# Row sums of a global attention spread by DMA copies in place of a matmul, with the steps behind them one slot later

## What is computed

```python
x = x + L0_conv_ref(_gn(x), ...)        # neighbourhood attention, 7x7 windows, 16 heads of 8 channels
t = _to_tokens(x)                       # (8, 3136, 128)
t = t + L1_attn_ref(_ln_t(t), ...)      # global attention, 8 heads of 16 channels, softmax over 3136 keys
t = t + L1_ffn_ref(_ln_t(t), ...)       # two linear maps without bias, the first one dequantised
x = _from_tokens(t, x)
```

## Time and profile before

| | |
|---|---|
| median of 3 runs | 9302.65 us (9293.14 to 9307.9) |
| span of the profiled execution | 9305.0 us |
| instructions | 435888 |
| mean granted TensorE clock, share of full speed | 0.979 |
| TensorE matmuls busy | 8705.1 us (94%), 173512 instructions |
| VectorE busy | 7484.8 us (80%) |
| ScalarE busy | 6697.0 us (72%) |
| GpSimd busy | 2837.7 us (30%) |
| DMA | 257.48 MB, mean 28 GB/s |

### The profile page before, as it was taken

One profiled execution on the slowest core, in us unless ns is written; L12 is line 12 of the kernel. 1 busy time (PEld: TensorE's weight loads), 2 busy tenths in 40 slices (PEclk: granted clock), 3 DMA queues, 4 the chain that ended last, 5 costly groups with the idle time before them and its releaser, 6 DMA issues.

```text
span 9305.0 us, 435888 instructions
## 1 busy us (share of the span) xinstructions
PE 8705.1 (94%) x173512; PEld 4692.7 (50%) x173512; DVE 7484.8 (80%) x13786; ACT 6697.0 (72%) x14241; POOL 2837.7 (30%) x2805
## 2 busy tenths in 40 slices
PE   5799999999999999999999999999999999999998
PEld 4445554555545555455554555545555455554543
DVE  6588888888787787888778877888778878789985
ACT  2377777777777777777777777777777777777777
POOL 5524441244303343034330343303432134320000
PEclk8899999999999999999999999999999999999999
DMA  1110101101011010110002000020011200011000
GB/s 44 45 43 20 28 25 41 26 21 27 24 43 26 18 28 24 48 25 20 23 25 55 16 21 24 25 52 17 22 27 27 49 14 25 25 27 30 8 11 8
DMA packets 312360, 257.48 MB, mean 28 GB/s; under 512 B 97244, under 2 KB 303052, under 8 KB 308300
## 3 DMA queue, kind: packets, MB, share of 16 engines
q1 hardware_dynamic: 310348, 229.05, 10.1%
HBM read 136.82 MB, written 78.05 MB: 23 GB/s over the span
## 4 chain that ended last, share of the span: by engine, by line
PE 87%; issue 5%; DVE 3%; ACT 2%; POOL 2%; DMA 1%; SPq 0%; ACTq 0%; DVEq 0%; POOLq 0%
PE PS L1156 23%; PE PS L1224 23%; PE PS L1209 22%; PE PS L966 6%; PE PS L1024 5%; PE PS L1032 4%; PE PS L1042 3%; ACT PB L1440 1%; DVE block_max L1694 1%; PE PS L1016 1%; PE PS L1072 1%; PE PS L998 0%; DVE X L1618 0%; DMA vT_padded<-SC 0%; DVE NM L1565 0%
## 5 line engine op out<-in xcount | busy, mean ns | idle before, releaser
L1694 DVE TENSOR_REDUCE block_max<-PS 128x1 f32<-128x448 f32 x10862 | 6160.8, 617 | 1098.6 <-PE PS L1156 1023.1
L1440 ACT ACTIVATE PB<-PS 128x448 f32<-128x448 f32 (+1 forms) x11200 | 5429.7, 545 | 1678.0 <-PE PS L1209 1645.8
L1209 PE MATMUL PS<-QP,KP 99*32 99x448 bf16 x43904 | 4261.6, 355 | 99.5 <-ACT PB L1440 50.3
L1156 PE MATMUL PS<-KP,QP 96*32 96x448 bf16 x43904 | 4230.6, 357 | 110.5 <-issue 63.3
L1224 PE MATMUL PS<-PB,VA 128*32 128x448 f32 x22400 | 2698.9, 543 | 1.6 <-issue 1.0
L1156 PEld LDWEIGHTS PS<-KP,QP 96*32 96x32 bf16 x43904 | 1389.2, 96 | 1627.2 <-DVE block_max L1694 747.3
L1209 PEld LDWEIGHTS PS<-QP,KP 99*32 99x32 bf16 x43904 | 1402.1, 97 | 1275.1 <-issue 500.4
L872 POOL TENSOR_TENSOR SC<-SC,NM 128x1120 f32<-128x1120 f32 x210 | 433.1, 2062 | 1793.9 <-DVE NM L1565 1793.9
L1224 PEld LDWEIGHTS PS<-PB,VA 128*32 128x32 f32 x22400 | 775.8, 111 | 300.8 <-issue 11.0
L846 POOL TENSOR_TENSOR QB<-Qn,C 128x896 f32<-128x896 f32 x392 | 662.1, 1710 | 11.6 <-ACT Qn L1298 11.6
L1024 PE MATMUL PS<-KR,QB 128*32 128x80 f32 x21952 | 537.6, 235 | 71.5 <-issue 23.1
(11 more groups left out here) (115 smaller groups left out, 4648.7 us busy)
## 6 DMA issues: line engine op xcount, KB each, us to landing
QP<-q_dram SPq DMA_DIRECT2D x672, 56.0 KB, 2.1
VP<-vT_padded SPq DMA_DIRECT2D x448, 70.0 KB
k_dram<-k_parts SPq DMA_DIRECT2D x56, 336.0 KB, 2.8
KP<-k_dram SPq DMA_DIRECT2D x336, 56.0 KB, 2.0
q_dram<-q_parts SPq DMA_DIRECT2D x56, 336.0 KB, 3.6
KP<-k_dram SPq DMA_DIRECT2D x48, 392.0 KB, 6.0
VA<-v_dram SPq DMA_DIRECT2D x16, 816.0 KB, 4.4
vT_padded<-SC SPq DMA_DIRECT2D x112, 112.0 KB
```

What stands on the lines that cost most here:

```text
L1156: ins = mm(PS[at:at + QT, bank, 0:BLK], QP[0:ROWS, Q_SLOTS[k % AUNITS], t:t + QT], KP[0:ROWS, g, t // BLK, j * BLK:(j + 1) * BLK], start=T ...
L1209: ins = mm(PS[k0:k0 + 32, bank, 0:BLK], KP[0:ROWSM, k // NBLK, h, c * P + k0:c * P + k0 + 32], QP[0:ROWSM, Q_SLOTS[k], h * BLK:(h + 1) * B ...
L1440: S.activation(exp_buffer(k, c)[0:n, h, :], PS[0:n, at % ST_BANKS, 0:BLK], ACT.Exp, scale=float(ADIM) ** -0.5).then_inc(exp_done, 1)
L1694: V.tensor_reduce(block_max[:, k % 2, q, j:j + 1], PS[:, bank, 0:BLK], AX.X, ALU.max).then_inc(max_read, 1)
```

## The change

The matmul `spread` is taken out, with its constant. In its place SP copies the row sum of each of the four heads to that head's 32 partitions of `tail[:, 1, :]`, by four DMAs from SBUF to SBUF with a source that is repeated 32 times. ScalarE's Ln reads this instead of PSUM. The wait for the last norm's readers of `tail[:, 1, :]` moves from ScalarE to SP. The copies stand in slot 1, sub 0; the inversion and all that follows it, the last norm too, stand one slot later. Side tasks that the planner puts into free places move where such a place was taken or came free.

```diff
-               "q2": "act", "v2": "dve", "spread": "act", "project": "dve", "mean3": "dve", "var3": "act",
+               "q2": "act", "v2": "dve", "project": "dve", "mean3": "dve", "var3": "act",
...
-            self.fix(t + 1, 1, "spread", k)
-            self.fix(t + 1, 1, "invert", k)
-            self.fix(t + 2, 1, "normalise_unit", k)
-            self.fix(t + 3, 1, "project", k)
+            self.fix(t + 1, 0, "spread_sums", k)
+            self.fix(t + 2, 1, "invert", k)
+            self.fix(t + 3, 1, "normalise_unit", k)
+            self.fix(t + 4, 1, "project", k)
             if k == 0 or k > NBLK:
                 i = (k - 1 - NBLK) % NBLK
-                self.fix(t + 5, 1, "mean3", i)
-                self.fix(t + 6, 0, "square3", i)
-                self.fix(t + 7, 1, "var3", i)
-                self.fix(t + 9, 0, "scale3", i)
-                self.fix(t + 10, 1, "ffn", i)
-                self.fix(t + 12, 0, "store_out", i)
+                self.fix(t + 6, 1, "mean3", i)
+                self.fix(t + 7, 0, "square3", i)
+                self.fix(t + 8, 1, "var3", i)
+                self.fix(t + 10, 0, "scale3", i)
+                self.fix(t + 11, 1, "ffn", i)
+                self.fix(t + 13, 0, "store_out", i)
...
-    c = np.zeros((P, 2 + 4 * P + GH + 1 + NHEADS), np.float32)
+    c = np.zeros((P, 2 + 3 * P + GH + 1 + NHEADS), np.float32)
...
-    c[:, 3 * P:4 * P] = p[:, None] == 32 * (p[None, :] // 32) + ADIM
...
-            if task == "spread":
-                return sums_log, of(b, 0, AUNITS, i)
...
+                def spread_sums(k):
+                    arrived(attn_read, of(b, 0, AUNITS, k))
+                    arrived(attn_normed, of(b, 0, AUNITS, k - 1))
+                    arrived(normed3, thirds_before(b, k))
+                    for h in range(GH):
+                        row = 32 * h + ADIM
+                        src = tail[row:row + 1, 0, :].rearrange("p (o t) -> p o t", o=1).to_broadcast([1, 32, BLK])
+                        sp.dma_start(tail[32 * h:32 * h + 32, 1, :], src).then_inc(sums_spread, 16)
...
-                def spread(k, bank):
-
-                    pe.wait_ge(attn_read, of(b, 0, AUNITS, k))
-                    across(bank, pick_sum, tail[:, 0, :]).then_inc(sums_spread, 1)
...
-                    act.wait_ge(sums_spread, of(b, 0, AUNITS, k))
-                    wait(act, normed3, thirds_before(b, k))
-                    S.activation(tail[:, 1, :], PS[:, SIDE_BANK, 0:BLK], ACT.Ln).then_inc(sums_log, 1)
+                    act.wait_ge(sums_spread, of(b, 0, AUNITS * 64, k * 64))
+                    S.activation(tail[:, 1, :], tail[:, 1, :], ACT.Ln).then_inc(sums_log, 1)
```

More of the change, by code:

```diff
@@ L284, in shape_constants @@
     c[:, 2 * P:3 * P] = (p[:, None] // 4 == p[None, :] // 4) / 4.0
-    c[:, 3 * P:4 * P] = p[:, None] == 32 * (p[None, :] // 32) + ADIM
-    c[:, 4 * P:4 * P + GH] = (p[:, None] % 32) // NDIM == np.arange(GH)[None, :]
-    c[:, 4 * P + GH] = 1e-5
+    c[:, 3 * P:3 * P + GH] = (p[:, None] % 32) // NDIM == np.arange(GH)[None, :]
+    c[:, 3 * P + GH] = 1e-5
     c[:, -2] = p % (QI * QJ) < QJ
     c[:, -1] = p % (QI * QJ) >= QJ
-    c[:, 4 * P + GH + 1:4 * P + GH + 1 + NHEADS] = p[:, None] // NDIM == np.arange(NHEADS)[None, :]
+    c[:, 3 * P + GH + 1:3 * P + GH + 1 + NHEADS] = p[:, None] // NDIM == np.arange(NHEADS)[None, :]
     return c
@@ L367, in hybrid_block @@
         ident, mean_w = C[:, 0:P], C[:, P:2 * P]
[L368 to L371, removed]
+        group_w = C[:, 2 * P:3 * P]
+        head_mask = C[:, 3 * P:3 * P + GH]
+        eps5 = C[:, 3 * P + GH:3 * P + GH + 1]
+        own_head = C[:, 3 * P + GH + 1:3 * P + GH + 1 + NHEADS]
         W_qkv = sb("W_qkv", [P, 3 * P])
@@ L762, in do @@
                         send_shift(i)
+                    elif task == "spread_sums":
+                        spread_sums(i)
                     elif task == "copy_x":
@@ L1131, in do @@
                         v2(i, bank)
-                    elif task == "spread":
-                        spread(i, bank)
                     elif task == "project":
```

## The result

The changed kernel takes 9819.4 us (median of 4 runs, 9806.26 to 9827.22); the kernel before, beside it, 9304.0 us (4 runs, 9293.14 to 9307.9). The ratio is 1.0545, with a 95% interval of 1.0527 to 1.0563: 515 us slower. The direction was forecast; the size, 9450 us with a range of 9170 to 9700, was not. The nearest of the cases written down is "one after the other", 9793 us, which had 0.16. The profiled execution has a span of 9824.4 us, and its mean granted clock is 0.960 in place of 0.979.

What follows compares the result with a forecast made beforehand. TensorE sets the pace; -93 us without a wait, +196 for late copies, +34 for the clock and +6 at the end give +143 on 9305: 9448, say 9450 us, range 9170 to 9700.

Steps and rivals of the forecast that it cites:

- one after the other: Rival: a unit's four copies run serially, landing at 9.3 us; +488 us, 9793 us; chance 0.16 including slower.
- The copies are held by their one source partition: SP's copies: reading one partition limits the rate; 1.8 us a copy, between 0.45 and 7.2 us.
- I take 7.5 us: Last copy's landing after the row sums; late by 1.47 us in 90 units, 3.04 in 21: 196 us.
- two by two: Rival: a unit's copies run in pairs, last landing at 6.6 us; +23 us, 9328 us; chance 0.12.
- the 21 units: Last image and last unit of seven others: TensorE stops long enough to drop its clock, 1.6 us each, 34 us.
- -93 us without a wait: Whole kernel without late copies: 84 us of matmul and 62 of stall saved, 53 given back.
- The stall in that slot goes: Slot 1, TensorE: 0.55 us of stall vanishes with the 0.75 us spread in 112 units; the stall is 62 us.
- The pair in slot 2: ScalarE's Ln and Exp, one slot later and no longer partly covered by the spread: 0.47 us a unit, 53 us.
- Moved: nothing: Product, projection, last norm, store and twelve planner tasks in later or neighbouring slots: no cost, about 20 us at worst.
- SP's queue: SP has time for the copies; a copy queued behind slot 24's key load costs at most 28 us.
- in time: Rival: copies land in 3.6 to 4.4 us, so no wait; 9214 us, down to 9170; chance 0.36.
- The gain is given back at another engine: Rival: VectorE takes over in slot 1, the 62 us stay; 9280 us with copies in time; inside the first rival.

Runs made afterwards that it cites:

- e2: The changed kernel without its four copies, Ln reading a constant tile of ones: 9318.2 us, ratio 0.9988 to the kernel before.
- e3: The changed kernel with each copy reading 32 partitions of a constant tile instead of one partition 32 times: 9373.22 us, ratio 1.0039.
- e6: The changed kernel with each copy writing 16 rows for each head in place of 32: 9374.46 us, ratio 1.0075.
- e8: The changed kernel with the heads' copies issued in the order 0, 2, 1, 3: 9575.35 us (one run).
- e13: The kernel before, nothing moved, its spread matmul shrunk from 448 columns to one and Ln reading a constant: 9248.05 us, ratio 0.9951.
- e1: The kernel before, with its spread matmul and everything behind it one slot later, no copies: 9362.99 us, ratio 1.0031.
- e14: The kernel before with the one-column spread and Ln of a constant, plus Exp split off into slot 2, sub 0: 9213.58 us, ratio 0.9910.
- e9: The changed kernel without copies (Ln of a constant), with the last norm back in its old slots: 9281.34 us, ratio 0.9982.
- e11: The changed kernel without copies, last norm in its old slots, Exp split off into slot 3, sub 0: 9295.01 us, ratio 0.9973.
- e12: The changed kernel with 16-row copies ordered 0, 2, 1, 3, norm in old slots, Exp split off, second unit one slot later: 9345.42 us, ratio 1.0029.
- e10: The kernel before with its inversion split, Ln still in slot 1, Exp in slot 2, sub 0: 9302.48 us, ratio 0.9982.

## Why the prediction was wrong in size, step by step

The sum as measured, against the kernel before on the same chip: no copies, -11 us (e2); copies from a wide source, 55 more, +44 (e3); one source partition, 471 more, +515. Of the 471, ScalarE's wait is 328.4 - 24.2 = 304 us. The clock: (1 - 0.960) x 9824.4 x 2 = 786 us were worked at half clock, against (1 - 0.978) x 9375.8 x 2 = 412 in e3; 374 us more, of which half is lost, 187. Together 491, a little over the 471. (The changed kernel stands against 9304.0 us, e2 and e3 against 9329.37; the kernel before differs that much from chip to chip.)

- **What bounds the kernel, and which wait would take over**: right. TensorE stands for ScalarE, ScalarE for the copies, in 105 of 112 units. The spread's rows fell by the 896 instructions named, and slot 1 of the last image takes 2.29 us where "about 2.3" was said. The slack, read from one unit each, was right too: in e2, with no copy to wait for, Ln starts 6.0 us after the row sums in the mean of the middle units and 4.2 in the last image, where 6.03 and 4.46 were said.
- **The copies are held by their one source partition**: right, and shown by e3 and e6. The 1.8 us a copy was right by luck: it is the middle of a factor of 16 between two ends. No copy was measured alone; the first two of a unit, which come from 16 and 48, land 4.3 us after their first packet starts, 2.15 us a copy.
- **"I take 7.5 us" to the last landing**: the step that failed first. ScalarE went on 8.47 us after the row sums. An issue takes 0.59 us, not 0.45, so the fourth is issued at 2.12 us, not 1.45; and "they should overlap more" was wrong for the order used, whose neighbours share a way out. The 7.2 us that the prediction names beside its own 7.5 is for both ways out at work at once, and e8, whose order has them so, came to 6.88. At 8.47 it is nearer to the 9.3 us of one after the other than to the 6.6 of two by two. With it the wait was 328 us, not 196: in a sum that goes with what exceeds a slack of 6.03 or 4.46 us, one more us of landing is 111 us more.
- **The clock, 34 us in "the 21 units"**: the second. I took a stop to count only from the 2.3 us seen in the earlier trace rows and gave the 90 middle units 1.47. With the copies a microsecond later 72 of the units had a wait of over 2.5 us at ScalarE, and 69 of these a stretch at half clock. The 187 us over 72 stops are 2.6 us for each, not 1.6. The term should have been tied to the landing time: at 8.47 us it is most units, not 21.
- **-93 us without a wait**: the third, measured -11. The starts of the weighting matmuls tell where it went, e2's profile less that of the kernel before, summed over the 112 units: slot 1 -119 us (forecast -146), slot 2 +40 (forecast +53), slots 3 and 4, between which the projection moved, +27, slot 0 -18, slots 5 to 13 +40, slots 14 to 24 +34 (forecast for all of these: nothing). The sum, +4, is some 15 us above what the medians say: beside e2 the kernel before took 9329.37 us, and its profile is of a run of 9305. (a) "The stall in that slot goes", 1.30 us in all 112 units, was read in the last image, and there slot 1 did fall from 3.59 to 2.26 us. In the middle images it fell from 4.08 to 3.05. Nor does the stall hang on the spread alone: in place, the matmul's removal gave 47 us, since Ln and Exp still stand in one piece, as the 0.44 us in e13 show; with these split, 81. (b) The pair in slot 2 was priced at 0.47 a unit and cost 0.36 in the middle images and 0.43 in the last: right. (c) "Moved: nothing", at worst 20 us: e1 measured 34. The two single edits add up, -47 + 34 = -13 against e2's -11. By e1's profile the 34 us lie in the slots to which the spread, the pair and the projection moved (+34 in slots 0 to 4) and less in those of the norm (+15).
- **SP's queue**: the right queue in the wrong direction. I feared a copy behind a load; in fact a store that the side work waits for stood behind the copies: 58.7 to 88.7 us of waiting from e2 to e3, 102.6 in the changed kernel. "It has time" looked only at the loads behind the copies, not at the stores.
- **The rivals**: "in time" (0.36) was priced at 9214; without any copy the kernel takes 9318.2 (e2), and with copies that land in 2.0 us 9373.22 (e3). That case would have been a loss too, or at best no gain. "One after the other" was near in its time, 9793, and its sign, a dip of the clock in most units, was seen; but the number is near by luck, since in it a wait of 396 us (measured 328) stands against a gain of 93 (measured 11). "The gain is given back at another engine" was dismissed for VectorE; in part it did happen, at ScalarE: the 35 us between e13 and e14.

**Left open.** In e2, e9, e11 and e12 TensorE has more idle time whose end no wait explains (total us, times, longest). The kernel before, e1 and e2:

```profile
PE PS L1156 <- issue: 63.3, 28, 9.3
```

```profile
PE PS L1156 <- issue: 60.0, 30, 9.3
```

```profile
PE PS L1152 <- issue: 92.4, 64, 9.1
```

e13, which keeps the instruction in place, stays at the first value (59.4, 27 times). Summed over all its waits, TensorE's idle time put down to issue is 219 us before, 225 in e1, 223 in e13 and 261 in e2 (251 in e9, 278 in e11). Where in a unit the kernels lose shows by the starts of the weighting matmuls (us, summed over the 112 units, against the kernel before):

| run | spread matmul | slots 0 to 4 | slots 5 to 13 | slots 14 to 24 |
|---|---|---|---|---|
| e1 | there | +34 | +15 | -3 |
| e10 | there | -12 | -3 | +3 |
| e13 | one column | -60 | -3 | -7 |
| e14 | one column | -72 | -18 | -7 |
| e2 | gone | -70 | +40 | +34 |
| e9 | gone | -67 | +4 | +27 |
| e11 | gone | -73 | +38 | +36 |
| e3 | gone | -16 | +50 | +34 |

Nothing of a unit's end stands in slots 14 to 24, and yet all ten kernels without the matmul lose 20 to 37 us there, and the four that keep its instructions between -7 and +3; e1 and e2 ran on one chip, e10 and e11 on another. So about a third of the forecast gain is lost far from the slots that the edit touches, part of it with no wait of the program. It is not the twelve side tasks that the planner moves, since e1 moves the same twelve. What it is was not tested: the stream of instructions on TensorE is another one, and the tile of constants is 128 columns smaller. The 34 us of e1 are of another make, since its issue time hardly grew and its slots 14 to 24 lost nothing, and that -47 and +34 add up to e2 is then partly chance. Nor was the inversion tried two slots later than in the changed kernel with copies of 32 rows.

## What to carry to other kernels

Price a DMA by its source as well as its size: a broadcast from one partition landed in 5.0 us where the same bytes from 32 partitions took 2.0, and an order in which neighbouring copies shared a way out cost 234 us. Where the margin is thin, do not write one landing time but the slope, here 111 us for each us, and put the clock's price on the same slope: here 304 us of waiting brought 187 us of clock with them. To learn what an instruction costs before rebuilding the schedule around its absence, shrink it in place to one column; and look at what stands behind it on the engine that waited, since that may be what ends last. Read a slot in every kind of stretch before multiplying it by all units: the last image gave 1.33 us, the middle ones 1.03.

## What was not expected of the hardware

- The order of four copies from partitions 16, 48, 80 and 112 was worth 234 us (one run): with 16 next to 48 and 80 next to 112 a unit's packets take 6.6 us, with 16 next to 80 they take 5.0, that is 46 GB/s for the 229,376 B. The Trainium skill, SBUF — State Buffer, "Door 1: The DMA port swizzle", gives 27.2 GB/s for a port, by which a copy of 57,344 B is an estimated 2.1 us. No run here measured one alone; the 2.15 us a copy of the first two of a unit agree with it.
- With the copies the longest tenth of all packets of 1792 B takes 0.93 us and more; in the kernel before the median of that size is 0.074 us and the longest takes 0.53.
- An issue on SP of an SBUF to SBUF copy was 0.59 us in the median, also for the wide source (590 in both), against 0.375 for a load of the same size. A row of six loads right behind the copies took 6.59 us to issue (the timeline above), where 2.80 us is what six take in e13.
